# A decoder layer's cross attention: layer norms on ScalarE, VectorE's small work moved, three stacked places

## Chip, cores and metric

One core of a Trainium2 chip runs the whole layer in one program. The metric is the device time in microseconds. Engines are named as in the profile: PE (TensorE), DVE (VectorE), ACT (ScalarE), POOL (GpSimd), SP (the queue that issues most DMAs). They run their own instruction lists and meet only at semaphores.

## The reference

Inputs are x (32 batches x 100 tokens x 256 channels) and a context (32 x 361 x 192). Three stages add to x:

```python
x = x + recurrent_mixer(layernorm(x))            # 4 heads, scan over tokens
x = x + cross_attention(layernorm(x), context)   # 16 heads of 16 channels, 361 keys
x = x + experts(layernorm(x))                    # 8 experts, top 2 of each token

def cross_attention(query, key_value):           # the stage of this change
    q, k, v = query @ Wq + bq, key_value @ Wk + bk, key_value @ Wv + bv   # by heads
    attn = softmax(clip((q @ k.T) * 0.25, -10000, 10000))
    return (attn @ v) @ Wo + bo
def layernorm(x): return (x - mean(x)) / sqrt(var(x) + 1e-5)
def experts(x):  # logits = x @ Wr.T; top 2; softmax of the two weights; gated MLP of each chosen expert
```

## The kernel before

Three functions follow each other: stage_mixer, stage_attention, stage_experts. Only stage_attention is touched. Its loop `every_batch` (L805) is unrolled over 32 batches on each engine; a body has four quarters t = 0 to 3, one for each four heads (n = 4b + t numbers the quarters). The order of each engine's work is written out by hand in its `body`.

**One batch.** The layer norm of the query stream is done two batches ahead: DVE bn_stats and bn_aggr (`moments`), POOL adds eps and takes the power -0.5 (`norm`), DVE applies it (`norm`, L1321), PE turns the result (`turn`), ACT copies it, PE multiplies for q. Keys are multiplied by PE into bank_m (`keys`, L1499) in two halves c = 0, 1 at quarters 2 and 3, copied by ACT to kf (L1193) and then to a bf16 high part (`keys_high`, L1199). For exact scores from bf16 products q and k are each split into three bf16 parts: ACT makes the high one, POOL the middle and the low one (`split_k`, three passes a half, L1056 to L1060; `split_q`). SP then stacks the parts: `stack` (L957) issues 12 small DMAs into k_st and 12 into q_st (L963), 16 rows each, for 96 rows of contraction. k_st and q_st have two places, batch parity; stack(b+1) waits until the scores of batch b-1 are done (L965).

**Scores, twice.** `scores` (L1536) gives queries x keys in bank_s for two heads (a pair) at a time; DVE takes the negated maximum (`maxima`, L1327) and, after the second pair, clips four of them (`negated`, L1332). bank_s is a single buffer: each pair waits for the maximum of the pair before (max_done). `scores_t` (L1544) gives keys x queries in bank_st, three key tiles of four heads. DVE clips them (`clip`, L1338); POOL spreads the maxima on a diagonal (`diag`, L1075); PE adds them (`shift`, L1553); ACT takes exp (L1220); PE weighs the values (`weigh`, L1564) one quarter later.

**A batch later**, b-1: PE turns the sums back (`back_turn`), DVE divides (`normalise`), PE turns the heads (`out_turn`, L1580), ACT adds the bias (L1233), PE projects (`out_project`, L1586), DVE adds the residual (`residual`, L1433, in quarter 2), and takes the moments for the third layer norm (`moments3`); POOL makes its rstd (`norm3`, L1048), DVE applies it into row (`norm3`, L1362), in quarter 3. **Two batches later**: PE turns the row (`turn3`, quarter 0), routes (`route`), DVE finds the best two experts (`best_two`). For each pair of batches `one_hots`, `count` (PE, L1607, at the end of odd batches) and `place` (DVE, L1395 to L1401, at the start of even ones) find the slot of each token, and POOL sends rows to slots with indirect DMAs (`send`, L1122). bank_m serves keys, back_turn, out_turn, projection, turn3, route and count in turn, and each use waits for the reader of the one before.

At the end `tile_map` (DVE) computes for each tile of 128 slots its expert and its row.

The first scores of a batch are issued in quarter 3 of the batch before, after waits for both stacks:

```python
if t == 0 and pair == 0:
    pe.wait_ge(k_stacked, STACKED * (b + 1))
    pe.wait_ge(q_stacked, STACKED * (b + 1))
after(pe, max_done, 2 * n + pair)
```

Of the kernel before, what the change touches and what calls it, by code (L numbers as in the profile page):

```python
# [17 lines left out]
ALU = mybir.AluOpType  # L18
# [797 lines left out]
def stage_attention(nc, w, x1, w1, w1_loaded, w2, w2_loaded, ident, slot_rows, out, out_stored, tile_expert, tile_row):  # L816
# [9 lines left out]
    with ExitStack() as ctx:  # L826
# [3 lines left out]
        def sem(name):  # L830
# [20 lines left out]
        rstd = sb("xrstd", [T, 1])  # L851
# [8 lines left out]
        q_st = sb("q_st", [96, 2, NH, T], BF16)  # L860
        k_st = sb("k_st", [96, 2, NH, S], BF16)
# [11 lines left out]
        moment3 = sb("moment3", [T, 3])  # L873
# [24 lines left out]
        needs = sb("needs", [1, E, EXPERT_TILES])  # L898
# [4 lines left out]
        skipped = sb("skipped", [1, TILES, E])  # L903
# [15 lines left out]
                 "top_done index_done index_f_done gap_done gap_exp_done den_done3 first_done hot_done pairs_done "  # L919
# [9 lines left out]
         top_done, index_done, index_f_done, gap_done, gap_exp_done, den_done3, first_done, hot_done, pairs_done,  # L929
# [14 lines left out]
        def _(sp):  # L944
# [12 lines left out]
            def stack(b, p):  # L957

                def spread(dst, part, slots, parts, c, done):
                    for slot in slots:  # L960
                        row = 16 * slot

                        sp.dma_start(dst[row:row + 16, p, 8 * c:8 * c + 8], part[:, parts, c]).then_inc(done, 16)  # L963

                until(st_summed, 12 * (b - 1))  # L965
                until(s_summed, 8 * (b - 1))
# [36 lines left out]
            def body(b, q, i):  # L1003
# [3 lines left out]
                if more_than(b, 1):  # L1007
                    stack(b + 1, 1 - p)
# [15 lines left out]
        def _(pool):  # L1024
# [15 lines left out]
            def norm(b):  # L1040
                pool.wait_ge(mv_done, b + 1)
                pool.tensor_tensor(rstd[:], mean_var[:, 1:2], eps[:], ALU.add).then_inc(eps_added, 1)
                pool.wait_ge(eps_added, b + 1)
                pool.tensor_tensor(rstd[:], rstd[:], power[:], ALU.pow).then_inc(rstd_done, 1)

            def norm3(b):
# [3 lines left out]
                pool.tensor_tensor(moment3[:, 2:3], moment3[:, 2:3], power[:], ALU.pow).then_inc(rstd3_done, 1)  # L1050

# [134 lines left out]
        def _(act):  # L1186
# [59 lines left out]

            def second_row(b, q):
# [10 lines left out]
            for b in (0, 1):  # L1258
                keys(b, 0)
# [9 lines left out]
            def body(b, q, i):  # L1269
                first = isinstance(b, int) and b == 0  # L1270
                routed = not (isinstance(b, int) and b < 2)
                for t in range(4):
# [13 lines left out]
                    exps(4 * b + t, t)  # L1286
                    if t == 0 and routed:
# [13 lines left out]
            heads_turn(BATCH - 1)  # L1301
            turned3(BATCH - 1)
# [4 lines left out]
        def _(dve):  # L1307
# [5 lines left out]
            def moments(b):  # L1313
                dve.bn_stats(stats[:], stream(b)).then_inc(stats_done, 1)
# [3 lines left out]

            def norm(b):
                dve.wait_ge(rstd_done, b + 1)  # L1320
                dve.tensor_scalar(xn[:], stream(b), mean_var[:, 0:1], rstd[:, 0:1], ALU.subtract,  # L1321
                                  ALU.mult).then_inc(xn_done, 1)
# [33 lines left out]

            def norm3(b, q, i):

                dve.wait_ge(rstd3_done, b + 1)
                if q % 2 == 0:  # L1360
                    after(dve, scattered[q // 2], SENT * i)
                dve.tensor_scalar(row[:, q // 2, q % 2, 0, 0:D], stream(b), moment3[:, 0:1], moment3[:, 2:3],  # L1362
                                  ALU.subtract, ALU.mult).then_inc(xn3_done, 1)
# [39 lines left out]
            def tile_map():  # L1403
# [3 lines left out]
                def then(ins):  # L1407
# [3 lines left out]

                dve.wait_ge(totalled, 1)
                then(dve.tensor_copy(n_rows[:], bank_v[0:1, 0:E]))
                then(dve.tensor_tensor(needs[:], n_rows[:].unsqueeze(2).to_broadcast([1, E, EXPERT_TILES]),
                                       iota_full[:].unsqueeze(1).to_broadcast([1, E, EXPERT_TILES]), ALU.is_gt))
                then(dve.tensor_reduce(n_tiles[:], needs[:], AX.X, ALU.add))
# [4 lines left out]
                then(dve.tensor_tensor(skipped[:], past[:], skip[:].unsqueeze(1).to_broadcast([1, TILES, E]),  # L1421
                                       ALU.mult))
                then(dve.tensor_reduce(row_f[:], skipped[:], AX.X, ALU.add))
# [573 lines left out]
```

## Time and profile before

| | |
|---|---|
| median of 3 runs | 1612.8 us (1611.31 to 1620.85) |
| profiled execution | 1611.83 us, span 1609.9 us |
| granted PE clock, mean | 0.953 |
| stages | mixer to about 489 us, attention to about 1247, experts to the end |

The span runs from the first to the last instruction of the profile. Busy time is time in which an engine worked on an instruction; "[0.96 <-DVE neg_raw L1327]" behind a row of a timeline says that the engine stood idle for 0.96 us before it and that the last thing it waited for was DVE's line 1327. Groups of like instructions are merged in a timeline (x2, x12).

### The profile page before, as it was taken

The numbers are of one execution on the slowest core, as the hardware profiler recorded it, in microseconds if no ns is written. First come the engines' busy times: TensorE is split into PE (matmuls) and PEld (weight loads), VectorE is DVE, ScalarE is ACT, GpSimd is POOL, SyncE is SP. The second block draws the span as 40 slices with busy tenths as digits, with TensorE's granted clock in tenths as the row PEclk, the third lists the DMA queues.
The fourth block names the chain that finished last, engine by engine and source line by source line (L and its number), as shares of the span: only waits on it lengthen the run. The fifth ranks groups of instructions, "written<-read, shape, count | busy, mean of one in ns | idle before, by whom it ended". The sixth has DMA issues, their size and how long they took to land. (4 is left out here: it accounts for less than half of the span.)

```text
span 1609.9 us, 31655 instructions
## 1 busy us (share of the span) xinstructions
PE 1367.0 (85%) x9914; PEld 947.0 (59%) x9915; DVE 1020.0 (63%) x2361; ACT 553.0 (34%) x1356; POOL 786.4 (49%) x1072
## 2 busy tenths in 40 slices
PE   4788778877746998999998899999986699999996
PEld 2455555545534666666666666666664366666664
DVE  2687987798741777888787888888875122222221
ACT  1333323323311345444354444444442112122221
POOL 3234643463343557766666666777664122222222
PEclk9999999999975899999899999999995799999999
DMA  4992000000005655656555564655551122222222
GB/s 148 304 321 60 1 1 1 0 0 1 1 0 92 93 85 106 117 113 107 109 103 115 109 113 96 111 117 118 112 110 38 39 45 44 46 46 46 44 45 23
DMA packets 180329, 128.01 MB, mean 80 GB/s; under 512 B 69010, under 2 KB 173090, under 8 KB 180194
## 3 DMA queue, kind: packets, MB, share of 16 engines
q1 hardware_dynamic: 167890, 112.23, 33.0%
q0 software_dynamic: 12304, 14.10, 5.8%
q8 instruction: 70, 1.15, 0.4%
q14 instruction: 65, 0.53, 0.1%
HBM read 36.10 MB, written 44.83 MB: 50 GB/s over the span
## 5 line engine op out<-in xcount | busy, mean ns | idle before, releaser
L1327 DVE TENSOR_REDUCE neg_raw<-bank_s 100x2 f32<-100x722 f32 x256 | 231.0, 902 | 97.4 <-PE bank_s L1536 86.5
L1220 ACT ACTIVATE prob<-bank_st 120x400 f32<-120x400 f32 (+1 forms) x384 | 166.3, 512 | 190.1 <-PE bank_st L1553 190.1
L1877 POOL DMA_INDIRECT out<-result,target x57 | 88.2, 1547 | 266.6 <-DVE result L1851 263.7
L1338 DVE TENSOR_SCALAR bank_st<-bank_st 120x400 f32<-120x400 f32 (+1 forms) x384 | 195.3, 570 | 0.2 <-issue 0.2
L748 PE MATMUL bank_l<-q_heads,k 128*100 128x192 f32 (+4 forms) x512 | 119.3, 372 | 65.4 <-DVE attn L562 52.2
L1075 POOL TENSOR_TENSOR neg_diag<-xident_b,neg_max 100x400 bf16<-100x400 bf16 x128 | 109.4, 855 | 124.7 <-DVE neg_max L1332 116.4
L1862 DVE TENSOR_TENSOR hidden<-silu,ebank_v 128x512 f32<-128x512 f32 x57 | 39.2, 688 | 196.7 <-PE ebank_v L1786 196.7
L1536 PE MATMUL bank_s<-k_st,q_st 96*100 96x361 bf16 x512 | 130.6, 337 | 35.0 <-DVE neg_raw L1327 21.4
L748 PEld LDWEIGHTS bank_l<-q_heads,k 128*100 128x100 f32 x512 | 79.0, 172 | 113.8 <-DVE attn L562 43.2
L396 ACT ACTIVATE q_heads<-q 32x192 f32<-32x192 f32 (+3 forms) x168 | 62.1, 370 | 224.4 <-DVE q L521 221.4
L1544 PEld LDWEIGHTS bank_st<-q_st,k_st 96*120 96x120 bf16 (+1 forms) x1536 | 109.9, 137 | 22.2 <-ACT prob L1220 10.9
L1544 PE MATMUL bank_st<-q_st,k_st 96*120 96x100 bf16 (+1 forms) x1536 | 118.9, 222 | 0.7 <-ACT prob L1220 0.3
L1786 PE MATMUL ebank_g<-expert_w,rows_t 128*128 x228 | 109.9, 605 | 1.2 <-DVE rows_t L1842 0.8
L272 POOL TENSOR_TENSOR mixed<-part,xn_t 128x400 f32<-128x400 f32 x80 | 78.9, 1012 | 61.7 <-DVE part L438 61.7
L1805 PE MATMUL ebank_y<-residual,hidden_t 128*128 x456 | 108.0, 380 | 0.9 <-ACT hidden_t L1833 0.9
L1786 PE MATMUL ebank_v<-expert_w,rows_t 128*128 x228 | 107.9, 596 | 0.0
L1499 PE MATMUL bank_m<-kv,xw_k 96*128 96x361 f32 x256 | 95.6, 498 | 12.1 <-DMA kv<-in_ctx_t 10.3
L1833 ACT ACTIVATE hidden_t<-ebank_h 128x512 f32<-128x512 f32 x57 | 34.0, 597 | 198.0 <-PE ebank_h L1796 198.0
L1524 PE MATMUL bank_v<-xw_v,kv 96*120 96x256 f32 (+1 forms) x384 | 99.9, 399 | 1.4 <-ACT xval L1238 0.7
L1564 PE MATMUL bank_o<-prob,xval 120*32 120x100 f32 (+1 forms) x3072 | 95.0, 257 | 0.1
L1553 PE MATMUL bank_st<-neg_diag,xones_b 100*120 100x400 bf16 (+1 forms) x384 | 90.6, 341 | 2.1 <-DVE bank_st L1338 1.4
L278 POOL TENSOR_TENSOR gn_rstd<-gn_mv,eps 100x16 f32<-100x16 f32 x8 | 2.4, 300 | 179.2 <-DVE gn_mv L575 179.2
(203 smaller groups left out, 2724.7 us busy)
## 6 DMA issues: line engine op xcount, KB each, us to landing
k_st<-k_part SPq DMA_DIRECT2D x384, 90.2 KB
slot_rows<-empty SPq DMA_DIRECT2D x9, 2967.0 KB, 26.3
q_st<-q_part SPq DMA_DIRECT2D x384, 25.0 KB
kv<-in_ctx_t SPq DMA_DIRECT2D x32, 270.8 KB
expert_w<-in_w SPq DMA_DIRECT2D x16, 512.0 KB, 4.1
rows<-slot_rows SPq DMA_DIRECT2D x57, 129.0 KB
residual<-in_w SPq DMA_DIRECT2D x16, 256.0 KB, 4.5
residual<-in_x SPq DMA_DIRECT2D x8, 400.0 KB
```

Of the source, the lines that this page charges most:

```text
L748: pe.matmul(bank[0:T, at:at + RH * cols], k[:, p, j, 0:T], q_heads[:, lv % 2, :, j, 0:cols], start=True, stop=True).then_inc(level_summed, 1)
L1075: pool.tensor_tensor(neg_diag[:, t % 2], ident_b[:].unsqueeze(1).to_broadcast([T, 4, T]), neg_max[:, 4 * t:4 * t + 4].unsqueeze(2).to_broa ...
L1220: act.activation(prob[0:KEYS[c], t % 2, c], bank_st[c][0:KEYS[c], 0:4 * T], ACT.Exp).then_inc(exp_done, 1)
L1327: dve.tensor_reduce(neg_raw[:, h:h + 2], bank_s[0:T, :, 0:S], AX.X, ALU.max, negate=True).then_inc(max_done, 1)
L1338: dve.tensor_scalar(tile, tile, CLAMP, -CLAMP, ALU.min, ALU.max).then_inc(clipped, 1)
L1499: mm = pe.matmul(bank_m[:, 0:S], w_k[:, i, c * 128:(c + 1) * 128], kv[:, p, i], start=(i == 0), stop=(i == 1))
L1524: mm = pe.matmul(bank_v[0:KEYS[c], (c % 2) * D:(c % 2 + 1) * D], kv[:, p, i, KEY0[c]:KEY0[c] + KEYS[c]], w_v[:, i], start=(i == 0), stop=( ...
L1536: mm = pe.matmul(bank_s[0:T, i, 0:S], q_st[:, p, h], k_st[:, p, h], start=True, stop=True)
L1544: mm = pe.matmul(bank_st[c][0:KEYS[c], j * T:(j + 1) * T], k_st[:, p, h, KEY0[c]:KEY0[c] + KEYS[c]], q_st[:, p, h], start=(j == 0), stop=F ...
L1564: mm = pe.matmul(bank_o[32 * j:32 * j + 32, t * T:(t + 1) * T], val[0:KEYS[c], p, c, 17 * (4 * t + j):17 * (4 * t + j) + 32], prob[0:KEYS[ ...
L1786: mm = pe.matmul(dst[:], rows_t[:, u, c], w1_of[:, bass.ds(expert, 1), c, half * F:(half + 1) * F].rearrange("p o f -> p (o f)"), start=(c ...
L1805: mm = pe.matmul(bank_y[:, 0:D], hidden_t[:, u, f], w2_of[:, bass.ds(expert, 1), f].rearrange("p o d -> p (o d)"), start=(f == 0), stop=(f ...
```

## The change

- ACT gets `norm` (after the exponentials of quarter 1) and `norm3` (after those of quarter 3, before the second key half); they disappear from DVE. x * rstd - mean * rstd replaces (x - mean) * rstd, so POOL computes one more column, -mean * rstd.
- DVE: moments runs three batches ahead at the end of quarter 3, residual stands at the end of quarter 1, moments3 and one_hots at the end of quarter 2, place in quarter 0 behind the first maximum. Each quarter is maximum, clips, maximum, small work.
- PE: the count moves from the end of an odd batch into quarter 0 of the next, behind scores_t; turn3 moves behind the second scores of quarter 0.
- k_st and q_st have three places (b % 3), and stack(b) waits for the scores of batch b-3.
- tile_map computes the experts first and reuses one buffer.

```diff
-        q_st = sb("q_st", [96, 2, NH, T], BF16)
-        k_st = sb("k_st", [96, 2, NH, S], BF16)
+        q_st = sb("q_st", [96, 3, NH, T], BF16)
+        k_st = sb("k_st", [96, 3, NH, S], BF16)
...
@@ SP @@
-                until(st_summed, 12 * (b - 1))
-                until(s_summed, 8 * (b - 1))
+                until(st_summed, 12 * (b - 2))
+                until(s_summed, 8 * (b - 2))
...
-                    stack(b + 1, 1 - p)
+                    stack(b + 1, (b + 1) % 3)
@@ POOL @@
             def norm(b):
                 pool.wait_ge(mv_done, b + 1)
+                after(pool, xn_done, b)
...
+                pool.wait_ge(rstd_done, b + 1)
+                pool.tensor_scalar(rstd[:, 1:2], mean_var[:, 0:1], rstd[:, 0:1], -1.0, ALU.mult,
+                                   ALU.mult).then_inc(offset_done, 1)
             def norm3(b):
...
+                pool.wait_ge(rstd3_done, b + 1)
+                pool.tensor_scalar(moment3[:, 3:4], moment3[:, 0:1], moment3[:, 2:3], -1.0, ALU.mult,
+                                   ALU.mult).then_inc(offset3_done, 1)
@@ ACT @@
+            def norm(b):
+                act.wait_ge(offset_done, b + 1)
+                after(act, xn_turned, b)
+                act.activation(xn[:], stream(b), ACT.Identity, bias=rstd[:, 1:2], scale=rstd[:, 0:1]
+                               ).then_inc(xn_done, 1)
+
+            def norm3(b, q, i):
+                act.wait_ge(offset3_done, b + 1)
+                if q % 2 == 0:
+                    after(act, scattered[q // 2], SENT * i)
+                act.activation(row[:, q // 2, q % 2, 0, 0:D], stream(b), ACT.Identity, bias=moment3[:, 3:4],
+                               scale=moment3[:, 2:3]).then_inc(xn3_done, 1)
...
                     exps(4 * b + t, t)
+                    if t == 1 and more_than(b, 2):
+                        norm(b + 2)
+                    if t == 3 and not first:
+                        norm3(b - 1, (q - 1) % 4, i if q else i - 1)
@@ DVE @@
             def moments(b):
+                after(dve, offset_done, b)
...
-                    if t == 0 and p == 0 and not (isinstance(b, int) and b < 4):
-                        place(2 * i - 2 + q // 2, q // 2)
-                    if t == 1 and not (isinstance(b, int) and b < 2):
+                    if t == 1 and b >= 2:
                         best_two(b - 2, p, 2 * i - 1 + q // 2)
                     if go:
                         maxima(n + 1, (t + 1) % 4, 0)
-                    if more_than(b, 2) and t == 1:
-                        moments(b + 2)
-                    if t == 2 and p == 1 and not (isinstance(b, int) and b < 3):
-                        one_hots(2 * i - 1 + q // 2)
-                    if t == 2 and not first:
-                        residual(b - 1, 1 - p)
-                    if t == 3 and not first:
-                        moments3(b - 1)
+                    if t == 0 and p == 0 and b >= 4:
+                        place(2 * i - 2 + q // 2, q // 2)
                     for c in range(3):
                         clip(n, c)
-                    if t == 1 and not first:
+                    if t == 1 and b:
                         normalise(b - 1)
-                    if more_than(b, 2) and t == 1:
-                        norm(b + 2)
-                    if t == 3 and not first:
-                        norm3(b - 1, (q - 1) % 4, i if q else i - 1)
                     if go:
                         maxima(n + 1, (t + 1) % 4, 1)
                         negated(n + 1, (t + 1) % 4)
+                    if t == 1 and b:
+                        residual(b - 1, 1 - p)
+                    if t == 2 and b:
+                        moments3(b - 1)
+                    if t == 2 and p == 1 and b >= 3:
+                        one_hots(2 * i - 1 + q // 2)
+                    if t == 3 and more_than(b, 3):
+                        moments(b + 3)
@@ PE @@
                     for c in range(3):
-                        scores_t(n, p, t, c)
-                    if t == 0 and routed:
-                        if p == 0 and not (isinstance(b, int) and b < 4):
-                            pe.wait_ge(chosen_done, 2 * i - 1 + q // 2)
-                        if more:
-                            turn3(b - 2, (q - 2) % 4, k_done, CC * (b + 2))
...
+                        scores_t(n, b % 3, t, c)
+                    if t == 0 and p == 0 and b >= 4:
+                        count(2 * i - 2 + q // 2, k_done, CC * (b + 2))
...
                     if go:
-                        scores(nb, np_, nt, 1)
+                        scores(nb, nb % 3, nt, 1)
+                    if t == 0 and routed:
+                        if p == 0 and b >= 4:
+                            pe.wait_ge(chosen_done, 2 * i - 1 + q // 2)
+                        if more:
+                            turn3(b - 2, (q - 2) % 4, k_done, CC * (b + 2))
...
-                    if t == 3 and p == 1 and not (isinstance(b, int) and b < 3):
-                        if more2:
-                            count(2 * i - 1 + q // 2, k_done, CC * (b + 3))
...
             last = BATCH // 2 - 1
+            count(last - 1, x_done, BATCH - 1)
```

## Rows read from the trace of the kernel before

**Rows 1.** The page: busy time, share of the span and instructions by engine.
```profile
PE 1367.0 (85%) x9914; PEld 947.0 (59%) x9915; DVE 1020.0 (63%) x2361; ACT 553.0 (34%) x1356; POOL 786.4 (49%) x1072
```

**Rows 2.** One stretch: its us, busy time of PE, PEld, DVE, ACT, POOL, clock, DMA, GB/s.
```profile
800.00:900.00 100.00, 91.50 (x995) 68.18 (x994) 79.42 (x169) 47.59 (x129) 68.90 (x107) 1.00 0.53 107
```

**Rows 3.** Waits of PE between 600 and 1100 us: total us, times, longest us.
```profile
PE bank_s L1536 <- DVE neg_raw L1327: 13.9, 21, 1.6
PE bank_s L1536 <- DMA q_st<-q_part: 9.1, 13, 1.4
PE bank_m L1607 <- ACT kf L1193: 8.3, 12, 0.7
PE bank_m L1580 <- DVE heads L1345: 7.7, 21, 0.7
PE bank_m L1586 <- ACT heads_t L1233: 3.6, 22, 0.2
```

**Rows 4.** Timeline of PE: first scores of two batches, 15 batches apart.
```profile
828.46 0.48 PE L1536 MATMUL bank_s<-k_st,q_st 96*100 96x361 bf16 x2 [0.17 <-DVE neg_raw L1327]
...
1157.69 0.48 PE L1536 MATMUL bank_s<-k_st,q_st 96*100 96x361 bf16 x2 [0.59 <-DVE neg_raw L1327]
```

**Rows 5.** Timeline of DVE, end of one batch: start us, us, the rest.
```profile
717.64 1.49 DVE L1362 TENSOR_SCALAR row<-residual,moment 100x256 f32<-100x256 f32 x1
719.05 0.89 DVE L1327 TENSOR_REDUCE neg_raw<-bank_s 100x2 f32<-100x722 f32 x1
```

**Rows 6.** All instructions of three lines: ns min/median/max, first and last start.
```profile
L1362 DVE TENSOR_SCALAR row<-residual,moment x32: 404/1400/1502, 563.9 to 1235.5; 100x256 f32<-100x256 f32 x32
...
L1250 ACT ACTIVATE row<-row x32: 408/448/450, 572.6 to 1236.9; 100x256 f32<-100x256 f32 x32
...
L1103 POOL TENSOR_SCALAR den<-gap_exp x16: 227/242/244, 619.0 to 1240.1; 100x2 f32<-100x2 f32 x16
```

**Rows 7.** Timeline of PE, the end of one batch.
```profile
714.21 0.48 PE L1536 MATMUL bank_s<-k_st,q_st 96*100 96x361 bf16 x2 [0.32 <-DVE neg_raw L1327]
...
720.00 0.51 PE L1536 MATMUL bank_s<-k_st,q_st 96*100 96x361 bf16 x2 [0.96 <-DVE neg_raw L1327]
```

**Rows 8.** Timeline of ACT, the same place.
```profile
715.25 0.54 ACT L1199 ACTIVATE k_part<-kf 128x361 bf16<-128x361 f32 x1
717.87 1.29 ACT L1220 ACTIVATE prob<-bank_st 121x400 f32<-121x400 f32 x3 [2.08 <-PE bank_st L1553]
...
720.39 0.49 ACT L1199 ACTIVATE k_part<-kf 128x361 bf16<-128x361 f32 x1
```

**Rows 9.** Timeline of SP's queue, the stacking of one batch, and the shortest.
```profile
715.89 9.80 SPq L963 DMA_DIRECT2D k_st<-k_part  x12
...
725.80 8.65 SPq L963 DMA_DIRECT2D q_st<-q_part  x12
...
682.63 7.65 SPq L963 DMA_DIRECT2D q_st<-q_part  x12
```

**Rows 10.** Timeline of PE: first scores of a batch, behind the stacking.
```profile
692.62 0.48 PE L1536 MATMUL bank_s<-k_st,q_st 96*100 96x361 bf16 x2 [0.18 <-DMA q_st<-q_part]
...
735.98 0.48 PE L1536 MATMUL bank_s<-k_st,q_st 96*100 96x361 bf16 x2 [0.28 <-DMA q_st<-q_part]
```

**Rows 11.** Timeline of POOL, one pass of the key split.
```profile
722.88 0.87 POOL L1057 TENSOR_TENSOR k_part<-kf,k_part 128x361 bf16<-128x361 f32 x1
```

**Rows 12.** DVE and PE around 789 us, and the stretch after with its clock.
```profile
786.48 2.15 DVE L1401 TENSOR_TENSOR slots<-slot_f,first_slot 100x4 uint32<-100x4 f32 x1
...
779.82 0.48 PE L1536 MATMUL bank_s<-k_st,q_st 96*100 96x361 bf16 x2 [0.19 <-DMA q_st<-q_part]
...
789.50 0.51 PE L1536 MATMUL bank_s<-k_st,q_st 96*100 96x361 bf16 x2 [1.63 <-DVE neg_raw L1327]
...
792.00:796.00 4.00, 4.00 (x24) 3.27 (x23) 1.29 (x5) 2.14 (x6) 0.85 (x1) 0.50 0.36 71
```

More of the change, by code:

```diff
@@ L955, in load, with stack @@
                              ).then_inc(kv_loaded, 16)
-            def stack(b, p):
+            def stack(b, r):
                 def spread(dst, part, slots, parts, c, done):
@@ L961, in spread @@
                         row = 16 * slot
[L963 to L966 removed]
+                        sp.dma_start(dst[row:row + 16, r, 8 * c:8 * c + 8], part[:, parts, c]).then_inc(done, 16)
+                until(st_summed, 12 * (b - 2))
+                until(s_summed, 8 * (b - 2))
                 for c in range(CC):
@@ L1258, in _ @@
             for b in (0, 1):
+                norm(b)
                 keys(b, 0)
@@ L1301, in _ @@
             heads_turn(BATCH - 1)
+            norm3(BATCH - 1, 3, BATCH // 4 - 1)
             turned3(BATCH - 1)
@@ L1355, in moments3 @@
                 dve.bn_aggr(moment3[:, 0:2], stats3[:]).then_inc(mv3_done, 1)
[L1357 to L1363, printed above, removed]
             def best_two(b, j, h, bank=bank_m):
@@ L1428, in tile_map @@
                 then(dve.tensor_copy(tile_expert[:], expert_f[:]))
+                then(dve.tensor_tensor(past[:], past[:], skip[:].unsqueeze(1).to_broadcast([1, TILES, E]), ALU.mult))
+                then(dve.tensor_reduce(row_f[:], past[:], AX.X, ALU.add))
+                then(dve.scalar_tensor_tensor(row_f[:], iota_tile[:], 128.0, row_f[:], ALU.mult, ALU.add))
+                then(dve.tensor_copy(tile_row[:], row_f[:]))
             def residual(b, p):
@@ L1435, in _ @@
             moments(0)
-            norm(0)
             moments(1)
-            norm(1)
+            moments(2)
             maxima(0, 0, 0)
@@ L1480, in _ @@
             moments3(BATCH - 1)
-            norm3(BATCH - 1, 3, BATCH // 4 - 1)
             best_two(BATCH - 1, 1, last)
@@ L1526, in values, with scores @@
                 mm.then_inc(v_summed, 1)
-            def scores(b, p, t, pair):
+            def scores(b, r, t, pair):
                 n = 4 * b + t
@@ L1535, in scores, with scores_t @@
                     h = 4 * t + 2 * pair + i
-                    mm = pe.matmul(bank_s[0:T, i, 0:S], q_st[:, p, h], k_st[:, p, h], start=True, stop=True)
+                    mm = pe.matmul(bank_s[0:T, i, 0:S], q_st[:, r, h], k_st[:, r, h], start=True, stop=True)
                 mm.then_inc(s_summed, 1)
-            def scores_t(n, p, t, c):
+            def scores_t(n, r, t, c):
                 after(pe, exp_done, 3 * (n - 1) + c + 1)
@@ L1544, in scores_t @@
                     mm = pe.matmul(bank_st[c][0:KEYS[c], j * T:(j + 1) * T],
-                                   k_st[:, p, h, KEY0[c]:KEY0[c] + KEYS[c]], q_st[:, p, h], start=(j == 0),
+                                   k_st[:, r, h, KEY0[c]:KEY0[c] + KEYS[c]], q_st[:, r, h], start=(j == 0),
                                    stop=False, skip_group_check=True)
```

41 lines of the change are left out of this document (15 added, 26 removed).

## The prediction

> **What bounds the kernel now.** I read the page first: TensorE (PE) is busy 85% of the span, VectorE (DVE) 63%, ScalarE (ACT) 34%, GpSimd (POOL) 49% [rows 1]. Shares over the whole span mix three stages, and the diff touches only the middle one, so I then read one stretch inside it: 91.5 of 100 us for PE, 79.4 for DVE, 47.6 for ACT, 68.9 for POOL, granted clock 1.00 [rows 2]. PE has 8.5% left; no change of the other engines can win more than that of this stage. Third, PE's own waits there [rows 3]: 42.6 us in 500, in five kinds, three of them on DVE or ACT work that the change moves, one on the transfers into q_st, one on the two heads_t copies.
>
> The pace: from the first scores at 828.46 to those at 1157.69 there are 15 batches, 21.95 us each [rows 4]. So 500 us are 22.8 batches and the waits are 1.87 us a batch. Of that 39.0 us, 1.71 a batch, are of the four kinds that the change works on; the 0.16 of L1586 stays. **Floor of PE:** 21.95 - 1.71 = 20.24 us a batch.
>
> **Part 1, the norms leave VectorE.** norm3 (L1362) took 1.49 us at 717.64, and the maximum behind it, which frees bank_s, started at 719.05; the scores at 720.00 had waited 0.96 for it [rows 5, 7]. Its median is 1.40, though it is 0.40 at best with the same shape [rows 6]. ScalarE's price: a 100x256 activation from SBUF to SBUF took 0.45 (median of L1250) [rows 6]; twice a batch, 0.9 us on an engine 48% busy. POOL gets two one-column tensor_scalar, 0.24 each by L1103 [rows 6], behind its pow: 0.5 us a batch.
>
> Why 1.40 and not 0.40: in the timeline L1362 lies beside POOL's key split, a 0.87 us pass [rows 11]. The Trainium skill, SBUF — State Buffer, section Who interferes with whom, says that a tensor_scalar in a two-port mode and a GpSimd instruction exclude each other for the whole instruction. With the lone price VectorE would gain 0.8 us a batch, with the row's 1.40 + 0.40 = 1.8; I take 1.8, because it is what the row shows.
>
> **Part 2, VectorE's small work moved behind the quarter's maximum.** moments no longer stands before the clips of quarter 1, so normalise comes about 0.6 earlier and L1580's wait (7.7/21 = 0.37) goes. residual moves from quarter 2 to the end of quarter 1, behind a wait for out_summed. Queued behind it is the next maximum, which needs the scores that PE starts right after that projection and that take 0.5 us; residual takes 0.4, so I price it at nothing, or 0.1 if the cover is thin. moments3 and one_hots come earlier, which lets POOL's norm3 start without waiting in batches without sends. The S waits on DVE (the scores of the next batch, 0.2 to 0.6) go too.
>
> **Part 3, PE's order.** The count leaves the end of odd batches, where it waited 0.72 for ScalarE's kf (8.3/12), and comes after scores_t of quarter 0, about 1.1 us later. norm3 on ScalarE now stands before that kf, +0.45, so it arrives within 0.1 us of PE: no wait, at most 0.3. turn3 moves behind the second scores, past nothing that needs it before the route. tile_map does the same thirteen steps in another order in other memory: nothing. The added waits (offset_done, xn_turned, xn_done) are for work a quarter to a batch old.
>
> **Part 4, the third stacked place.** stack(b+1) no longer waits for the scores of batch b-1. But the key copy that starts it ended at 715.25 + 0.54 = 715.79, and the first k_st transfer was issued at 715.89 [rows 8, 9]. The copy, not the place, opens the stacking: alone, this part is worth 0 to 0.5 us, taken as 0. SP's order and its 24 issues stay; only the place index changes.
>
> **What is late next.** With the DVE waits gone, the first scores of a batch wait for q_st. Call their start S and follow the loop to the next batch's S:
> - S at 714.21 [rows 7]; the second key half's copy (L1199) ends at 720.39 + 0.49 = 720.88 [rows 8]: 6.67. norm3 now stands before it, behind the exponentials that start at 717.87: + 0.45.
> - SP then issues six k_st pieces. An issue costs 0.64 (12 in 7.65) [rows 9], six 3.83. Before, from 720.88 to the first q_st at 725.80 were 4.92 [rows 9], since POOL's middle part ended at 722.88 + 0.87 = 723.75 [rows 11]. POOL, no longer late with norm3, needs two passes of 0.87 from the copy, less than SP's first three issues (1.92). Plus 0.1 to start: 3.93.
> - Twelve q_st issues: 7.65 at best, 8.65 here [rows 9]; I take 8.2.
> - From the last issue to S: 692.62 - 690.28 = 2.34 and 735.98 - 734.45 = 1.53 [rows 9, 10]; I take 1.8, nearer to the more frequent small one.
>
> Sum: 6.67 + 0.45 + 3.93 + 8.2 + 1.8 = 21.05. The same sum for before is 6.67 + 4.92 + 8.2 + 1.8 = 21.59, where 21.95 was measured; the missing 0.36 is the later of several chains that vary. With one chain alone near the end I carry 0.15: **21.2 us a batch**, 0.75 less than now, and PE then waits about 1 us in each batch at S. So of the 1.71 that are freed less than half arrives. Ends of this term: 20.24 (PE's floor, all issues fast) and 21.95.
>
> **Sum.** 30 batches follow a first one: -22.5 us. Outside the loop the last norm3 and the first norm lie on the chain: activation for tensor_scalar and the extra POOL step, 2 x (0.05 + 0.24 + a wait of 0.1) = +0.8. The profiled execution took 1611.83 us (span 1609.9): 1590.1. The median of the runs, 1612.8, lies 1.0 above it: **1591**. A change of under 1% (16 us) can't be told from none here.
>
> **Rivals.**
> - *PE is the bound* (12%). If issues and landings keep to their short ends (7.65, 1.53) and the moved work covers, 6.67 + 0.45 + 3.93 + 7.65 + 1.53 = 20.23, PE's floor. Then 30 x 1.71 = 51 less, 1562. For it: issues at 0.64 do occur for twelve in a row [rows 9]. Against: q_st already ended last in 13 of 22 batches [rows 3].
> - *The chain is not shortened* (17%). norm3 in ScalarE's row and POOL's second step delay the key copy by more than POOL's earlier start returns; or place, now between a maximum and the clips, holds VectorE. The period is 21.5 to 21.95: 1599 to 1613, centre 1604.
> - *Slower: a blocked place drops the clock* (13%). Quarter 0 starts at S + 4.83 (720.00 less its wait of 0.96 [rows 7]); scores, scores_t, count and place's three steps take some 2.3 us, so L1401, the last of them (two inputs in SBUF), comes at about S + 7.1, just where POOL starts its key split (6.67 + 0.45). Once in 16 times it took 2.15 us, at 786.48; PE stood 1.63 at 789.50, and the granted clock was 0.50 from 792 to 796, the level of 1.2 GHz [rows 12]. From 779.82 to 828.46 two batches took 48.64, where two others take 43.9: 4.7 us lost. If the new place is caught in all its 14 turns inside the loop, 14 x 4.7 = 66 are lost, of which some 15 fall into PE's slack: 1591 + 51 = 1642. It decides once PE's idle in one piece passes about 1.6; gaps of 1.4 [rows 3] cost nothing beyond themselves. The same page of the Trainium skill says that a vector instruction with two SBUF inputs is shut out by a GpSimd one that reads SBUF; the row of 2.15 us agrees. For it speaks also the new wait of 1 us at S; against, that 15 of 16 were not caught.
> - That the change does not do what it says: the norms do leave VectorE by the diff; only the third place may do nothing, which the forecast already holds.
>
> **Chances.** Forecast (1583 to 1599) 58%, PE's floor 12%, no shortening 17%, slower 13%. Faster by over 1% (below 1596.7): most of the first and the second, 0.64; within 1%: the rest of the first and the third, 0.23; slower: 0.13. The range of 8 in 10 takes the forecast, the third case and the near part of the second: 1566 to 1612.
>
> **What would show it.** Right: the period between first scores near 21.2; L1536's wait for q_st near 1 us in nearly every batch and none for DVE; L1580 and L1607 without waits; DVE 7 to 8 us less busy per 100; k_st's first transfer still right behind the first key copy, and SP idle between the two key halves. Wrong: PE over 96% busy (floor), waits on DVE that remain at S, L1401 at 2 us, or stretches with clock 0.50 inside the loop.

## The result and the profile after

The changed kernel took 1630.9 us (median of 4 runs, 1627.8 to 1638.3), the kernel before 1612.4 on the same chip: ratio 1.0106, 95% interval [1.0078, 1.0135]. Slower by 18.5 us, where 1591 was forecast. The profiled execution took 1627.8 us, span 1625.9.

The page after, the line of busy times and the line of the granted clock in 40 slices:

```profile
PE 1389.1 (85%) x9914; PEld 975.7 (60%) x9915; DVE 992.0 (61%) x2297; ACT 578.3 (36%) x1420; POOL 799.6 (49%) x1136
PEclk9989999999866899999999999999986799999999
```

VectorE is 28 us less busy and ScalarE 25 us more, as the diff says [rows 1]. But PE is 22 us **more** busy with the same 9914 matmuls. More busy time for the same work is the first sign that the clock was lower. The stretch that was read before shows it (columns as in rows 2): the clock was 1.00 there and is 0.93 now, and fewer matmuls fit in [rows 2].

```profile
800.00:900.00 100.00, 92.15 (x964) 70.07 (x952) 73.89 (x158) 48.18 (x131) 68.47 (x116) 0.93 0.53 103
```

Waits of PE between 600 and 1100 us, then those of SP's queue for the parts of the keys that ScalarE (the high part) and POOL (the middle part) make (total us, times, longest us):

```profile
PE bank_s L1545 <- issue: 19.3, 11, 2.6
PE bank_s L1545 <- DMA q_st<-q_part: 14.1, 11, 2.1
PE bank_m L1595 <- ACT heads_t L1238: 5.9, 23, 0.3
PE bank_m L1616 <- ACT kf L1198: 1.2, 5, 0.2
```

```profile
SPq L947 <- ACT k_part L1204: 59.8, 34, 5.4
SPq L947 <- POOL k_part L1062: 26.9, 23, 1.9
```

The small waits on VectorE are gone [rows 3]: out_turn, which was L1580 and is L1589 now, is not in the list, and the count's wait for kf (L1616) fell from 8.3 us to 1.2. The wait for heads_t (L1595) grew from 3.6 to 5.9. In place of the rest stands one wait in each batch, at the first scores (L1545): 33.4 us in 22 batches, 1.52 each, up to 2.6. The total is 40.5 us where it was 42.6, so PE does not wait longer than before; but 33.4 of the 40.5 now lie in one piece a batch. The timeline of PE at two first scores, and what follows the second:

```profile
717.20 0.48 PE L1545 MATMUL bank_s<-k_st,q_st 96*100 96x361 bf16 x2 [1.37 <-DMA q_st<-q_part]
...
734.73 1.38 PE L1508 MATMUL bank_m<-kv,xw_k 96*128 96x361 f32 x4
...
738.46 0.81 PE L1545 MATMUL bank_s<-k_st,q_st 96*100 96x361 bf16 x2 [1.67 <-issue]
...
742.19 2.61 PE L1508 MATMUL bank_m<-kv,xw_k 96*128 96x361 f32 x4
```

The same key matmul takes 1.38 us ahead of the wait of 1.67 and 2.61 behind it. The stretches there, with the clock third from the right:

```profile
738.00:742.00 4.00, 3.54 (x40) 2.92 (x41) 2.36 (x4) 0.77 (x4) 3.73 (x8) 0.55 0.95 278
742.00:746.00 4.00, 4.00 (x15) 2.61 (x14) 1.59 (x4) 0.82 (x3) 1.82 (x3) 0.59 1.14 134
746.00:750.00 4.00, 3.89 (x55) 3.42 (x54) 2.61 (x7) 3.28 (x10) 1.25 (x2) 1.00 0.15 23
```

0.5 is the level of 1.2 GHz, 1.00 that of 2.4 GHz. Call S the start of a batch's first scores, and a stretch at the lower clock behind it a fall of the clock. Between the S at 563.19 and that at 1192.18 lie 28 batches. 10 of them have a fall; these took 24.0 us on average (22.8 to 25.1), the other 18 took 21.6. So a fall costs 2.4 us, and all 28 took 22.46 on average. Before, the 28 batches between the S at 560.43 and that at 1180.40 took 22.14: 26 of them 21.95 on average, one with a long fall 26.98 [rows 12], and the first, with a short one, 22.30.

That short fall of the kernel before is the one to look at. It lies outside the stretch that the prediction read (600 to 1100 us), behind a wait of PE for q_st at S. Timeline of PE before, and the clock there:

```profile
560.43 0.48 PE L1536 MATMUL bank_s<-k_st,q_st 96*100 96x361 bf16 x2 [1.44 <-DMA q_st<-q_part]
...
563.10 2.41 PE L1499 MATMUL bank_m<-kv,xw_k 96*128 96x361 f32 x4
```

```profile
560.00:564.00 4.00, 3.57 (x42) 2.85 (x43) 2.90 (x7) 0.88 (x3) 1.33 (x4) 0.72 0.88 234
```

It is the picture of 738.46 after the change, with a wait of 1.44 us and a shorter fall.

### The profile page after: what moved, and what is told of

Same layout as the page of the kernel before. It is cut to its first block and busy times, and to the rows that moved or that the text cites. A ratio compares the mean times of both kernels' runs of the same rounds, so it can differ in the third digit from the quotient of the medians.

```text
span 1625.9 us, 31779 instructions
## 1 busy us (share of the span) xinstructions
PE 1389.1 (85%) x9914; PEld 975.7 (60%) x9915; DVE 992.0 (61%) x2297; ACT 578.3 (36%) x1420; POOL 799.6 (49%) x1136
## 5 line engine op out<-in xcount | busy, mean ns | idle before, releaser
L1545 PE MATMUL bank_s<-k_st,q_st 96*100 96x361 bf16 x512 | 135.3, 348 | 48.2 <-issue 28.3
L748 PE MATMUL bank_l<-q_heads,k 128*100 128x192 f32 (+4 forms) x512 | 123.4, 382 | 61.5 <-DVE attn L562 49.5
L1553 PEld LDWEIGHTS bank_st<-q_st,k_st 96*120 96x120 bf16 (+1 forms) x1536 | 114.2, 142 | 23.9 <-ACT prob L1225 11.2
L1553 PE MATMUL bank_st<-q_st,k_st 96*120 96x100 bf16 (+1 forms) x1536 | 123.6, 227 | 0.7 <-ACT prob L1225 0.3
L1508 PE MATMUL bank_m<-kv,xw_k 96*128 96x361 f32 x256 | 106.8, 546 | 10.8 <-DMA kv<-in_ctx_t 10.1
L1545 PEld LDWEIGHTS bank_s<-k_st,q_st 96*100 96x100 bf16 x512 | 49.5, 130 | 80.2 <-issue 71.8
```

The source lines that it names most:

```text
L748: pe.matmul(bank[0:T, at:at + RH * cols], k[:, p, j, 0:T], q_heads[:, lv % 2, :, j, 0:cols], start=True, stop=True).then_inc(level_summed, 1)
L1508: mm = pe.matmul(bank_m[:, 0:S], w_k[:, i, c * 128:(c + 1) * 128], kv[:, p, i], start=(i == 0), stop=(i == 1))
L1545: mm = pe.matmul(bank_s[0:T, i, 0:S], q_st[:, r, h], k_st[:, r, h], start=True, stop=True)
L1553: mm = pe.matmul(bank_st[c][0:KEYS[c], j * T:(j + 1) * T], k_st[:, r, h, KEY0[c]:KEY0[c] + KEYS[c]], q_st[:, r, h], start=(j == 0), stop=F ...
```

## Experiments

Two theories at the outset. **Clock:** the change gathers PE's idle at S, and behind such a gap PE runs at the lower clock, as from 738 to 746 us above. **Chain:** the clock is a side effect; the loop from one key copy over SP to the next S has become longer by itself, through norm3 ahead of the key copy. All ratios are against the kernel before on the same chip; it took 1615 to 1617 us in these comparisons and 1612.4 in the first, so a difference of medians between the first comparison and these can be off by some 4 us, and the ratios are the better measure.

### e1_fill and e9_fill3: useless matmuls in the gap

Both compute what the changed kernel computes, with 256-column matmuls of no use in front of the waits for the stacks. The edit of e1_fill is shown; e9_fill3 has `range(3)`.

```diff
             def scores(b, r, t, pair):
+                after(pe, max_done, 2 * n + pair)
                 if t == 0 and pair == 0:
+                    for _ in range(5):
+                        pe.matmul(bank_s[:, 0, 0:D], w_q[:, 0, 0:128], w_q[:, 0], start=True, stop=True)
                     pe.wait_ge(k_stacked, STACKED * (b + 1))
                     pe.wait_ge(q_stacked, STACKED * (b + 1))
-                after(pe, max_done, 2 * n + pair)
```

> The changed kernel, and in front of the wait for the stacks at S (the first scores of a batch) PE runs five matmuls of 256 columns on weights into bank_s, some 1.1 us, whose result the scores overwrite. Clock theory: the changed kernel is slower because its waits are gathered into one idle of 1 to 2.75 us at S, after which the granted clock falls to 0.50 in 10 of its 30 batches; an interval between first scores takes about 21.6 us without and 24.1 with a fall. PE busy in that place keeps the clock: at most 2 falls in the loop, the q_st chain unchanged near 21.6 us a batch, time 1631 - 8 x 2.5 = about 1611 (1604 to 1616). Chain theory (the q_st chain alone sets the time, the clock's falls cost nothing because they hide in its slack): falls or none, the time stays at 1631 within 4 us. Extra-work theory (PE is bound by its work): 30 x up to 1.1 us more, above 1640.

Measured: 1628.6 us, 1.0078 [1.0054, 1.0102]. The granted clock did not fall once in the loop, but the time was missed: from the first of these five matmuls to the scores behind them pass 2.27 us (720.77 to 723.04), about twice what I had meant to add, and PE became the bound. Its wait for q_st shrank to 0.5 us in 500. So the run says that the falls end when the gap is filled, not yet what that is worth.

> The changed kernel with three matmuls of filler at S instead of five. Five filled 2.1 us (twice what was meant, longer than the idle of 1.5 us that they replaced) and PE itself became the bound of half of the batches; the clock never fell inside the loop. Three fill 1.3 us. Clock theory: no fall inside the loop, or at most two, the q_st chain again ends last at about 21.5 us a batch and the time is 1631 - 25 = about 1606 (1600 to 1612). If the idle itself and not the clock costs (PE has less to do than the chain takes), it stays near 1631.

Measured: **1606.1 us, 0.9945 [0.9923, 0.9967]**, as the clock theory had it. Timeline of PE, filler and first scores of two batches:

```profile
714.93 1.56 PE L1542 MATMUL bank_s<-xw_q 128*128 128x256 f32 x6 [0.65 <-DVE neg_raw L1351]
716.33 0.48 PE L1547 MATMUL bank_s<-k_st,q_st 96*100 96x361 bf16 x2
...
735.75 1.48 PE L1542 MATMUL bank_s<-xw_q 128*128 128x256 f32 x6
737.49 0.48 PE L1547 MATMUL bank_s<-k_st,q_st 96*100 96x361 bf16 x2 [0.25 <-DMA q_st<-q_part]
```

Stretch 800 to 900 us, for the clock, and PE's waits at S between 600 and 1100:

```profile
800.00:900.00 100.00, 95.70 (x1025) 74.26 (x1024) 75.72 (x166) 51.56 (x139) 72.86 (x119) 1.00 0.58 113
```

```profile
PE bank_s L1542 <- DVE neg_raw L1351: 6.2, 11, 0.7
PE bank_s L1547 <- DMA q_st<-q_part: 5.7, 11, 0.9
```

PE does about 1.5 us more work in each batch, no other engine's program is different, and the kernel is some 25 us faster than the changed one. There is no fall in the loop, and the batch takes 21.83 us, near the 21.6 of the changed kernel's batches without a fall. This shows the clock theory: without falls the chain of the changed kernel is shorter than that of the kernel before (21.6 us against 21.95), and what made the kernel slower is what PE's gap did to the clock.

### e2_late: the chain made shorter

ScalarE's norm3 moves from before the second key half's copy to behind it.

```diff
-                    if t == 3 and not first:
-                        norm3(b - 1, (q - 1) % 4, i if q else i - 1)
...
                     if more_than(b, 2) and t >= 2:
                         keys_high(b + 2, t - 2)
+                    if t == 3 and not first:
+                        norm3(b - 1, (q - 1) % 4, i if q else i - 1)
```

> The changed kernel, but ScalarE applies norm3 after the second key half, the queries and the key copy of quarter 3 instead of before them. Chain theory, part one: the q_st chain runs through the second key copy, which comes 0.5 us earlier, so an interval without a fall takes 21.1 instead of 21.6, PE's idle at S shrinks by 0.25 to 0.5 and the clock falls less often (3 to 7 instead of 10): 1631 - 15 - 10 = about 1606 (1600 to 1618). If the chain does not run through that copy (SP's 24 issues alone bound it): intervals unchanged, 1631 within 5.

Measured: 1618.2 us, 1.0011 [0.9986, 1.0036], 13 us faster than the changed kernel (15 by the ratios): at the upper edge of what the chain theory expected, and outside what its rival did. The wait at S went from 33.4 us to 29.0 in 500, and a batch takes 21.94 us instead of 22.46. But the 20 batches without a fall take 21.58 us, as in the changed kernel (21.61): the 21.1 that the chain theory expected did not come. What went are falls: 8 instead of 10, six of them about half as long, at 1.2 us each on average instead of 2.4. So e2_late gained through the clock and not through a shorter chain. The key copy did come 0.48 us earlier, but the first q_st transfer did not. The table under "Mis-sized" has the terms; why shorter waits at S came with an unchanged batch is not shown. PE's waits at S between 600 and 1100 us:

```profile
PE bank_s L1545 <- issue: 17.7, 12, 2.4
PE bank_s L1545 <- DMA q_st<-q_part: 11.3, 11, 1.4
```

### e3_before_three and e7_after_two: the third place alone

e3 is the kernel before with the third place and the new tile_map, e7 the changed kernel with two places. The edit of e3 is shown; e7's is the reverse.

```diff
-        q_st = sb("q_st", [96, 2, NH, T], BF16)
+        q_st = sb("q_st", [96, 3, NH, T], BF16)
...
-                until(st_summed, 12 * (b - 1))
-                until(s_summed, 8 * (b - 1))
+                until(st_summed, 12 * (b - 2))
+                until(s_summed, 8 * (b - 2))
...
-                    stack(b + 1, 1 - p)
+                    stack(b + 1, (b + 1) % 3)
```

> The kernel before with the third place of q_st and k_st alone (and the smaller tile_map that makes room for it). If the key copy opens the stacking, as the forecast had it: no change, within 4 us of before. If the wait for the scores of the batch before was a limit: the k_st issues start up to 0.5 us earlier, up to 15 us less.

> The changed kernel with two places instead of three. The stacking may then not begin before scores_t at S + 1.2, where the key copy comes at S + 0.4 (1.9 less PE's idle of 1.5 at S). If SP's idle between the key halves (about 2 us) takes that up, the time is that of the change within 5. If the third place is what holds the chain at 21.6, it is 30 x 0.8 = 24 slower, 1655.

Measured: e3 1613.4, 0.9972 [0.9952, 0.9992]; e7 1631.5, 1.0099 [1.0065, 1.0134], the ratio of the changed kernel. Before, the third place is worth 3 us by the medians, 1 to 8 by the interval; the loop of e3's profiled execution is not shorter (22.20 us a batch against 22.14), so where they come from is not shown. After, no difference is seen. In e3 the first k_st transfer is issued 0.1 us behind the first key copy in 27 of 28 batches: there the copy opens the stacking, as the prediction had it. In e7 it is issued 1.2 us behind it on average, up to 3.0, and in most batches 0.24 us behind the end of the scores_t that stack waits for, so there the scores open the stacking; SP's idle between the two key halves takes that up, as e7's expectation said it could.

### e8_norms_only: the norms alone

The kernel before with both norms on ScalarE and POOL's extra step; all orders stay.

```diff
@@ ACT @@
                     exps(4 * b + t, t)
+                    if t == 1 and more_than(b, 2):
+                        norm(b + 2)
+                    if t == 3 and not first:
+                        norm3(b - 1, (q - 1) % 4, i if q else i - 1)
@@ DVE @@
-                    if more_than(b, 2) and t == 1:
-                        norm(b + 2)
-                    if t == 3 and not first:
-                        norm3(b - 1, (q - 1) % 4, i if q else i - 1)
```

> The kernel before with the norms on ScalarE (and POOL's extra step) alone; order of VectorE and PE, and the two places, as before. Chain theory: VectorE's late maxima at S and at the end of a batch go, the count's wait for kf grows from 0.7 to 1.2 in odd batches, and the second key copy comes 0.5 to 0.6 us later, so that the q_st wait takes the place of what went: interval 21.7 to 22.1, the time within 8 of before. Forecast's own reading (1.8 us of VectorE freed shortens the batch by the 0.96 and 0.3 that PE waited): 10 to 20 less.

Measured: 1640.4 us, 1.0157 [1.0132, 1.0183], the slowest of all. PE's largest waits between 600 and 1100 us:

```profile
PE bank_s L1547 <- DMA q_st<-q_part: 19.8, 14, 2.1
PE bank_m L1618 <- ACT kf L1200: 12.0, 10, 1.2
PE bank_m L1591 <- DVE heads L1371: 7.0, 21, 0.7
```

The count, still at the end of the odd batch, waits for the kf that norm3 delays (8.3 us before, 12.0 now), and q_st is later: 19.8 us in 14 times instead of 9.1 in 13. Both readings that were expected missed. In the profiled execution, the fastest of the four (1631.5 us), 24 of 28 batches had no fall and took 22.3 us, where the kernel before has 21.95. So about 10 of the 16 us by which this loop is longer are not the clock's; the rest are four falls, one of them in a batch of 29.2 us, which I can't explain. How the other three executions divide is not known. By the medians the norms on ScalarE, with POOL's extra step, cost 24 us; the other parts of the change give back some 8 of them (1.0157 to 1.0106).

### e4_q6 and e5_before_q6: the chain cut

If SP's row of issues is what holds S, fewer issues must free it. q_st is laid out so that both halves of a slot go in one transfer: six transfers instead of twelve, the same bytes. e4 does it to the changed kernel, e5 to the kernel before.

```diff
+                def spread_q(slots, parts):
+                    for slot in slots:
+                        row = 16 * slot
+                        sp.dma_start(q_st[row:row + 16, r].rearrange("p (h c) t -> p h (c t)", c=CC),
+                                     q_part[:, parts].rearrange("p c t -> p (c t)")).then_inc(q_stacked, 16)
...
-                for c in range(CC):
-                    spread(q_st, q_part, (0, 1, 3), 0, c, q_stacked)
+                spread_q((0, 1, 3), 0)
...
-                    mm = pe.matmul(bank_s[0:T, i, 0:S], q_st[:, r, h], k_st[:, r, h], start=True, stop=True)
+                    mm = pe.matmul(bank_s[0:T, i, 0:S], q_st[:, r, h % 8 * 2 + h // 8], k_st[:, r, h], start=True, stop=True)
```

> The changed kernel, but q_st is laid out with the two channel halves of a head pair side by side, so that 6 DMAs of 128 pieces of 400 bytes do what 12 of 200 did. Chain theory: the q part of SP's issues shrinks from 8.2 to about 4 us, the chain falls to some 17.5 us, below PE's floor of 20.2; no idle at S, no falls inside the loop, 30 x 1.4 + 25 less: about 1565 (1558 to 1580). Clock theory alone (idle at S matters by whatever cause) expects the same. Against both: if the transfers' landing and not their issue were the limit, the idle at S stays over 1 us and the time at 1620 or more.

> The kernel before with the same six q_st DMAs. Its waits on DVE and ACT (1.33 us a batch) stay, only the q_st wait of 0.40 goes: the interval is about 21.5 instead of 21.95, 1612 - 30 x 0.4 = about 1600 (1594 to 1608). If the order of VectorE's work is what the change gains once the chain is out of the way, e4_q6 must be faster than this by some 30 us; if the change's order brings nothing, both are alike within 8.

Measured: **e4 1563.5, 0.9681 [0.9641, 0.9722]**; e5 1602.5, 0.9917 [0.9891, 0.9942]. SP's rows in e4, and PE's waits between 600 and 1100 us:

```profile
702.48 10.36 SPq L962 DMA_DIRECT2D k_st<-k_part  x12
712.95 5.00 SPq L967 DMA_DIRECT2D q_st<-q_part  x6
```

```profile
PE bank_s L1549 <- DVE neg_raw L1355: 7.2, 12, 0.8
PE bank_m L1599 <- ACT heads_t L1242: 5.9, 23, 0.3
PE bank_m L1620 <- ACT kf L1202: 3.1, 13, 0.2
PE bank_s L1549 <- issue: 2.0, 10, 0.2
```

Both came as expected. Twelve q_st issues took 8.54 us in the changed kernel, six take 3.8 to 5.2. The wait at S for q_st is gone, no fall is left in the loop, and a batch takes 20.42 us: the PE floor of the prediction was 20.24. Between e4 and e5 lies the change itself, and there it is worth 39 us, near the 30 x 1.33 = 40 of PE's waits that e5 keeps. So once q_st comes early the change gives what PE's small waits were worth; in the kernel as it stands, the chain over SP takes most of it away, and the clock takes more.

### e10_q6_send, e12_q6_apart, e6_late_q6, e11_q6_send_late: what is left in e4_q6

Batches of e4 alternate, 19.7 and 21.3 us. In the longer ones VectorE's maximum starts late. Timeline of e4 there, POOL, DVE and PE:

```profile
697.00 1.15 POOL L1131 DMA_INDIRECT slot_rows<-row,slots  x1 [0.21 <-issue]
...
697.99 0.51 PE L1549 MATMUL bank_s<-k_st,q_st 96*100 96x361 bf16 x2
698.46 0.99 POOL L1131 DMA_INDIRECT slot_rows<-row,slots  x1 [0.30 <-issue]
699.92 0.91 DVE L1355 TENSOR_REDUCE neg_raw<-bank_s 100x2 f32<-100x722 f32 x1 [0.75 <-PE bank_s L1549]
...
700.98 0.48 PE L1549 MATMUL bank_s<-k_st,q_st 96*100 96x361 bf16 x2 [0.57 <-DVE neg_raw L1355]
```

The scores ended at 698.50 and VectorE's clips at 699.17 (699.92 less 0.75), yet the maximum began at 699.92, after POOL's second indirect transfer had ended at 699.45. e10 puts the second send behind the diagonal of its quarter; e12 lets no two sends stand next to each other; e6 is e4 with e2's late norm3; e11 is both e10 and e6.

The edit of e10 against e4:

```diff
                 if sends:
                     send(h, hp, 0, 0)
-                    send(h, hp, 0, 1)
                 diag(b, 3)
                 if sends:
+                    send(h, hp, 0, 1)
                     send(h, hp, 1, 0)
```

> e4_q6 with the second of POOL's four indirect DMAs (send) issued behind the fourth diagonal instead of before it. In e4_q6 every second batch PE waits 0.6 us at S for VectorE's maximum, and that maximum starts 0.75 us late, 0.5 us after POOL has finished its second send, although its scores had been ready for over a microsecond. If the send holds VectorE: the maximum starts right behind the clips, PE's 0.6 goes, the longer intervals fall from 21.3 to about 20.6 and the time by 8 to 12 us, to 1553. If something else delays it: the 0.6 stays, 1563 within 4, or the longer wait of norm3 shows.

> e4_q6 with no two of POOL's indirect DMAs back to back: the second behind the fourth diagonal, the third behind norm3's small steps. In e10_q6_send the maximum behind the two separated ones started on time, and the one beside the two that had become neighbours started 1.0 us late. If two sends in a row hold VectorE's maximum, none is late now and the loop takes 20.2 to 20.4 us a batch instead of 20.42 (e4_q6) and 20.63 (e10): 1550 to 1560. If a single send is enough to hold it, or norm3's step comes too late, it stays at 1563 to 1570.

> e4_q6 with ScalarE's norm3 behind the second key copy, as in e2_late. With the q_st chain out of the way that order can only give the 0.23 us that the count waits for kf in every second batch: 3 us less, 1560, or nothing (the expectation of the chain theory: the 13 us of e2_late came from the chain and must not come again).

> Both together: 1550 if both hold (12 and 3 less than e4_q6), 1553 if only the send does.

Measured, against before: e10 1569.5, 0.9713 [0.9678, 0.9748]; e12 1562.8, 0.9676 [0.965, 0.9701]; e6 1571.2, 0.9724 [0.9687, 0.976]; e11 1576.0, 0.9763 [0.9732, 0.9794]. Of these only e11 is clear of e4 (0.9681 [0.9641, 0.9722]) by the intervals. None is faster: e10, e6 and e11 missed, and e12 lies between its two expectations. In e10 the maximum behind the single send came on time, and the next quarter, where two sends now stood together, had it late. Timeline of e10:

```profile
706.72 1.03 POOL L1131 DMA_INDIRECT slot_rows<-row,slots  x1 [0.18 <-issue]
708.05 0.99 POOL L1131 DMA_INDIRECT slot_rows<-row,slots  x1 [0.30 <-issue]
...
709.59 0.91 DVE L1355 TENSOR_REDUCE neg_raw<-bank_s 100x2 f32<-100x722 f32 x1 [1.01 <-PE bank_s L1549]
```

In e12 the late maximum at S is gone from the waits but for one of 0.3 us, the diagonals come late instead, and nearly every batch takes 20.46 to 20.52. So the late maximum moves and goes with the pairs of sends, as expected, but taking it away gains nothing. PE's waits of e12:

```profile
PE bank_st L1567 <- POOL neg_diag L1084: 4.1, 12, 0.4
PE bank_s L1550 <- DVE neg_raw L1356: 0.3, 1, 0.3
```

In e6 the late norm3 lets the key copy and with it POOL's key split come earlier, and the split now meets place. All instructions of the slots line, ns min/median/max, in e4 and then in e6:

```profile
L1421 DVE TENSOR_TENSOR slots<-slot_f,first_slot x16: 161/163/165, 606.2 to 1189.4; 100x4 uint32<-100x4 f32 x16
```

```profile
L1421 DVE TENSOR_TENSOR slots<-slot_f,first_slot x16: 161/1628/1861, 609.4 to 1201.6; 100x4 uint32<-100x4 f32 x16
```

This is the blocked place of the prediction's slower rival, in a kernel where it occurs nearly every time: 1.63 us instead of 0.16, starting 7.3 us behind S (the rival had said 7.1), beside two passes of the split. It brought no fall of the clock, where the rival had priced 51 us. e6's median lies 8 us above e4's, but that is not shown to be the price of place: place stands in the even batches, which take 21.1 us in e6 as in e4 (21.2), and the odd ones grew, from 19.7 to 20.2.

## Why the prediction was wrong

Its own steps, in order.

**Held.** VectorE's and PE's moved work: out_turn without a wait, the count's at 1.2 us in 500, none left on VectorE at S; no wait on residual shows. The third place: no difference after (e7), 3 us before (e3). The first k_st transfer 0.1 us behind the first key copy in most batches, and SP idle between the halves. The norms took 56 us from VectorE's row, 1.76 a batch where 1.8 was forecast. But VectorE is only 5.5 us less busy per 100 (79.4 to 73.9), not 7 to 8: `negated` (L1356), which now often lies beside a pass of POOL's key split, takes 0.36 us on average instead of 0.22, up to 1.27, which gives 18 us back. The chain's terms were near in a good batch. Rows of ACT and SP after the S at 717.20:

```profile
722.03 0.61 ACT L1266 ACTIVATE row<-residual,moment 100x256 f32<-100x256 f32 x1
...
723.87 0.49 ACT L1204 ACTIVATE k_part<-kf 128x361 bf16<-128x361 f32 x1
```

```profile
718.10 10.16 SPq L961 DMA_DIRECT2D k_st<-k_part  x12
728.37 8.54 SPq L961 DMA_DIRECT2D q_st<-q_part  x12
```

The key copy ends at 724.36, 7.16 behind S (forecast 7.12); the first q_st issue comes 4.01 later (3.93); twelve issues take 8.54 (8.2); the scores at 738.46 come 1.55 behind the last (1.8). Sum 21.26 in that batch, forecast 21.05 and 21.2 with what was carried. The S waits that a list of waits puts down to "issue" belong to this chain too: at the S at 738.46 and at nearly all others so marked the scores start 1.5 to 1.6 us behind the last q_st issue, like many of those put down to q_st, and the maximum before had ended 1.2 us or more earlier.

**Failed: "PE then waits about 1 us in each batch at S", taken to be harmless.** The forecast's sum has no term for what the clock does behind that wait. The rival had named the threat, "decides once PE's idle in one piece passes about 1.6", and that the new wait speaks for it, but let it come only with a blocked place and put 13% on that. The place stayed free after:

```profile
L1417 DVE TENSOR_TENSOR slots<-slot_f,first_slot x16: 161/162/832, 613.5 to 1257.1; 100x4 uint32<-100x4 f32 x16
```

What passed 1.6 us was the forecast's own wait, which averages 1.52 and spreads from 0.3 to 2.75. A mean of 1 us that varies should have been read against the same decision point. The premise "gaps of 1.4 [rows 3] cost nothing beyond themselves" was wrong too: rows 3 show waits, not what followed, and only from 600 us on; the kernel before has a fall behind a wait of 1.44 at 560.43, shown above. Nor is the point sharp: in the changed kernel falls followed waits of 1.41 (at 989.47) to 2.75 (at 1192.18), and none followed waits of 1.70, 1.83 and 2.37 at 674.82, 967.75 and 1057.11.

**Mis-sized.** (1) norm3 on ScalarE at 0.45 by L1250: it takes 0.61, norm 0.64, with the same shape; L1250 is a plain copy, these two have a scale and a bias column. The copy came only 0.48 later for it. The heads_t wait is 0.26 a time instead of 0.16. (2) The batch without a fall takes 21.6 us, not 21.2. The terms of the chain, as means over the batches without a fall:

| us | forecast | before (26) | changed (18) | e2_late (20) |
|---|---|---|---|---|
| S to the end of the second key copy | 7.12 | 6.67 | 7.15 | 6.67 |
| copy to the first q_st issue | 3.93 | 5.03 | 4.44 | 4.99 |
| twelve q_st issues | 8.2 | 8.31 | 8.39 | 8.27 |
| last issue to the next S | 1.8 | 1.94 | 1.63 | 1.66 |
| sum | 21.05, carried as 21.2 | 21.95 | 21.61 | 21.58 |

The term that was too small is the second. 4.0 is what it takes when all goes well, as in the batch above; on average its six k_st issues took 0.3 longer, and POOL's middle part came 0.1 late. e2_late shows how little the copy alone decides: there it came 0.48 earlier and the term grew by 0.55, since in the odd batches POOL began the split 0.97 us behind the copy, on average, instead of 0.39.

**The sum again.** The profiled execution was 37.7 us above the 1590.1 forecast for it. The forecast started from the kernel before, whose loop already holds 5.4 us of falls. So the falls inside the loop are 10 x 2.4 less 5.4, 18.6 us; the batches without a fall 28 x 0.41 = 11.5; the mixer, whose code did not change, ended 3.0 later (first keys at 501.16 instead of 498.14; in all these kernels that lies between 498 and 504). The last 5 us lie behind the S at 1192.18, with one more fall: that batch took 24.24 us, and 21.09 before. That is 38. And the 1% under which the prediction called a change not told from none was too wide: the interval of the ratio is 0.3% to either side. Falls are the largest term, and e9_fill3 shows it from the other side: 25 us back with the gap filled.

**The rivals.** The floor of PE did not come here, but e4_q6 reaches it within 0.2 us a batch once the chain is cut, at 1563.5 where the rival had said 1562. No shortening: its period, 21.5 to 21.95, holds the 21.6 of the 18 batches without a fall, and one of its two reasons is in the table, POOL's and SP's row behind the key copy; the other, a place that holds VectorE, did not come. Slower: right in its sign and in what kills the gain, wrong in its trigger. The Trainium skill's page SBUF — State Buffer, section Who interferes with whom, has a vector instruction with two SBUF inputs contend with a GpSimd one that reads SBUF. e6's rows for L1421 agree (1.63 us against 0.16), but in the changed kernel L1417 took 0.16 in the median, so this explains nothing of the 18.5 us here.

**Open.** Why equal waits sometimes bring a fall and sometimes not; why two indirect transfers in a row hold VectorE's maximum; why one S in two is put down to "issue" and not to q_st; what made e8 so slow in its other executions, and the odd batches of e6 longer than e4's.

## What to carry to other kernels

Removing several small waits of an engine that nearly bounds the kernel does not remove its idle if another chain is just behind: it gathers it in one place. In this kernel that place was worse than the many small ones, because the clock fell behind it. Before forecasting a gain, write down where the idle will lie in one piece, how much it varies, and what the trace, in all its stretches, shows of the clock behind gaps of that size. Then look at the chain that sets the gap first: here six transfers fewer in SP's queue (e4_q6) turned a loss of 1.1% into a gain of 3.2%.

## What was unexpected of the hardware

- Useless matmuls made a kernel faster: about 1.5 us of filler per batch took 25 us off 1631, with PE 95.7% busy (800 to 900 us) where it was 92.2.
- PE waited less in all than before the change (40.5 us in 500 against 42.6) and the kernel was slower: one wait a batch, of 1.5 us on average, came with 10 falls of the clock in 28 batches, several small ones with 2.
- One activation with a scale and a bias column takes 0.61 to 0.64 us at 100x256, the plain copy of L1250 0.45 [rows 6].
- Behind two indirect transfers of POOL that follow each other, VectorE's maximum starts about 0.5 us after the second has ended (699.45 to 699.92, 709.04 to 709.59), though its input had been ready for 0.75 to 1.0 us. In the loops of the changed kernel, e9, e4, e10 and e11 this holds for 62 of the 64 maxima whose input was ready during the second of two such transfers (0.4 to 0.9 us behind its end); maxima that were ready during a single or a first one began at once, in e12 too.
